# First layer: the heads' softmax denominators summed and inverted on 128 partitions and spread through DRAM

## What is computed

```python
x_flat = x.reshape(B, C, H * W).transpose(0, 2, 1)
Q, K, V = (split_heads(x_flat @ W + b) for W, b in ((Wq, bq), (Wk, bk), (Wv, bv)))
attn = softmax(einsum('bhnd,bhmd->bhnm', Q, K) * scale, axis=-1)
out = einsum('bhnm,bhmd->bhnd', attn, V)
out = out.transpose(0, 2, 1, 3).reshape(B, H * W, C) @ Wo + bo
y = out + x_flat
y = (y - mean(y)) / sqrt(var(y) + EPS) * gamma + beta      # over the channels
```

## Time and profile before

| | us |
|---|---|
| median of 3 runs | 5652.98 (5651.7 to 5654.66) |
| the profiled execution's own time | 5656.6 |
| its span, first to last instruction | 5654.8 |
| busy PE | 5338.5 (94% of the span) |
| busy DVE | 4949.7 (88%) |
| busy GpSimd | 4692.7 (83%) |
| busy ACT | 3876.3 (69%) |

### The profile page before, as it was taken

The page is one execution under the profiler, slowest core; times in us unless marked ns, Lnnn a source line. Parts: engine busy times, 40 slices in busy tenths (PEclk is TensorE's granted clock), DMA queues, the critical chain, the costliest instruction groups (busy, mean ns, idle before and its releaser), DMA issues. The chain is left out here.

```text
span 5654.8 us, 81519 instructions
## 1 busy us (share of the span) xinstructions
PE 5338.5 (94%) x25264; PEld 2432.7 (43%) x25264; DVE 4949.7 (88%) x7220; ACT 3876.3 (69%) x7513; POOL 4692.7 (83%) x3661
## 2 busy tenths in 40 slices
PE   7999999999999999999999999968888888888888
PEld 3444444444444444444444444423333333333333
DVE  6888888888888888888888888829999999999998
ACT  3666666666666766666666666657777777777776
POOL 4888887888888788888788888747888888888887
PEclk8999999999999999999999999989999999999999
DMA  4111122211111211112211010225555555555555
GB/s 139 36 53 50 37 61 71 60 55 38 46 49 64 79 39 53 45 40 62 64 54 33 18 32 21 67 84 196 186 190 188 188 187 189 186 188 190 186 188 174
DMA packets 337475, 549.14 MB, mean 97 GB/s; under 512 B 76016, under 2 KB 99568, under 8 KB 335600
## 3 DMA queue, kind: packets, MB, share of 16 engines
q1 hardware_dynamic: 327536, 526.62, 28.8%
q10 hardware_dynamic: 9504, 17.31, 1.1%
HBM read 415.10 MB, written 109.84 MB: 93 GB/s over the span
## 5 line engine op out<-in xcount | busy, mean ns | idle before, releaser
L649 DVE TENSOR_REDUCE mpart<-ps 128x1 f32<-128x512 f32 x4096 | 2539.1, 682 | 536.4 <-PE ps L406 535.8
L533 ACT ACTIVATE exps<-ps 128x512 f32<-128x512 f32 x4096 | 2146.8, 600 | 1139.8 <-PE ps L413 1114.1
L406 PE MATMUL ps<-k_st,q_ring 96*128 96x512 f32 x4096 | 1778.2, 435 | 20.2 <-DMA k_st<-qk_split 15.6
L413 PE MATMUL ps<-q_ring,k_st 98*128 98x512 f32 x4096 | 1621.5, 397 | 3.8 <-ACT exps L533 3.4
L1300 POOL TENSOR_TENSOR hc<-hh,c_rep 128x512 f32<-128x512 f32 x1024 | 1295.8, 1278 | 310.8 <-DVE hh L1269 291.8
L1269 DVE TENSOR_TENSOR_SCAN hh<-d_a,carry,ps 128x512 f32<-128x512 f32 x1024 | 1311.9, 1284 | 0.0
L622 POOL TENSOR_TENSOR held<-exps 128x512 f32<-128x512 f32 x768 | 987.7, 1311 | 359.9 <-ACT exps L533 359.9
L406 PEld LDWEIGHTS ps<-k_st,q_ring 96*128 96x128 f32 x4096 | 774.7, 189 | 1136.5 <-DVE mpart L649 685.2
L622 POOL TENSOR_TENSOR sums<-exps 128x512 f32<-128x512 f32 x896 | 1134.5, 1282 | 72.0 <-ACT exps L533 70.0
L424 PE MATMUL ps<-exps,v_ring 128*32 128x512 f32 x8192 | 1092.4, 605 | 0.0
L413 PEld LDWEIGHTS ps<-q_ring,k_st 98*128 98x128 f32 x4096 | 778.3, 190 | 139.7 <-ACT exps L533 18.0
(11 more groups left out here) (113 smaller groups left out, 3881.3 us busy)
## 6 DMA issues: line engine op xcount, KB each, us to landing
d_a<-dt_dram SPq DMA_DIRECT2D x1040, 256.0 KB
qk_split<-hilo SPq DMA_DIRECT2D x128, 256.0 KB, 2.3
out_dram<-out_sb SPq DMA_DIRECT2D x128, 256.0 KB, 2.0
heads_in<-out_dram SPq DMA_DIRECT2D x32, 1024.0 KB, 5.2
q_ring<-qk_split SPq DMA_DIRECT2D x384, 64.0 KB, 2.0
k_st<-qk_split SPq DMA_DIRECT2D x45, 512.0 KB, 7.4
dt_dram<-dt SPq DMA_DIRECT2D x33, 512.0 KB, 5.5
s_u<-lo_u ACTq DMA_DIRECT2D x66, 256.0 KB, 5.9
```

Source lines behind the costliest of these rows:

```text
L406: nc.tensor.matmul(d_bank(("max", m, t)), q_ring[0:PARTS, m % 4, 128 * i:128 * i + 128], k_st[0:PARTS, g % 2, chunk(kc)], start=True, stop ...
L413: nc.tensor.matmul(a_bank(("exp", n, t)), k_st[0:SHIFT, n // NCH % 2, 128 * t:128 * t + 128], q_ring[0:SHIFT, n % 4, :], start=True, stop= ...
L533: nc.scalar.activation(exps[:, u % EXPS, CH * half:CH * half + CH], a_bank(("exp", n, t)), ACT.Exp, scale=SCALE).then_inc(a_done, 1)
L649: nc.vector.tensor_reduce(mpart[:, m % 2, t % 4, t // 4:t // 4 + 1], d_bank(("max", m, t)), AX.X, ALU.max).then_inc(d_done, 1)
```

## The change

The denominators no longer go through `denom`, `sel_d` and PE. `store_den` writes a slot's four rows to a DRAM tensor `den_dram` in pieces of 16 columns. In a slot with f, `load_den` loads them as `den_in`, with the (head, piece) pair as the 128 partitions and 4 x 16 values in each. DVE sums the four parts and takes the reciprocal (`invert`, in quad v = 3, behind its quarter of `held`). SP stores the 128 x 16 result to `rec_dram`, waits until it has landed, and loads it to `recip` with each head's row repeated on its 32 partitions (`spread_rec`). PE's matmul and ACT's two activations go, and so does the key "den" in the ring `a_at`. ACT's copy of the denominators moves: it stands behind the first exp tile of quad v = 1, no longer behind the fourth, in all slots but the last.

```diff
-                if v == 4:
-                    add(a, ("den", f))
...
                 def store_den(n):
                     f = batch_of(n) * NCH + n % NCH
                     sp.wait_ge(den_read, n + 1)
-                    if f >= NCH:
-                        sp.wait_ge(a_ready, a_at["den", f - NCH] + 1)
-                    sp.dma_start(denom[row:row + 4, half, :], den_parts[::D, n % 2, :]).then_inc(den_stored[n % 2], 16)
+                    if f >= 2 * NCH:
+                        sp.wait_ge(den_loaded, 16 * (f - 2 * NCH + 1))
+                    sp.dma_start(den_dram[batch_of(n) % 2, n % NCH, n // NCH % HEADS, :, :, :].rearrange("k q l -> q k l"),
+                                 den_parts[::D, n % 2, :].rearrange("q (k l) -> q k l", k=32)).then_inc(den_stored[n % 2], 16)
+
+                def load_den(f):
+                    sp.wait_ge(den_stored[f % 2], 16 * (last_slot(f) // 2 + 1))
+                    if f:
+                        sp.wait_ge(den_summed, f)
+                    sp.dma_start(den_in[:, :, :], den_dram[f // NCH % 2, f % NCH, :, :, :, :].rearrange("h k q l -> (h k) q l")
+                                 ).then_inc(den_loaded, 16)
+
+                def spread_rec(f):
+                    sp.wait_ge(rec_ready, f + 1)
+                    if f:
+                        sp.wait_ge(recip_ready, 16 * f)
+                        sp.wait_ge(d_done, d_at["join", f - 1] + 1)
+                    sp.dma_start(rec_dram.rearrange("h (k l) -> (h k) l", k=32), rec[:, :]).then_inc(rec_stored, 16)
+                    sp.wait_ge(rec_stored, 16 * f + 16)
+                    sp.dma_start(recip[:, :], rec_dram.rearrange("h (o l) -> h o l", o=1).to_broadcast([HEADS, D, CH])).then_inc(recip_ready, 16)
...
-                def spread_den(f):
-                    row, half = den_rows(f)
-                    pe.wait_ge(den_stored[f % 2], 16 * (last_slot(f) // 2 + 1))
-                    a_room(("den", f))
-                    nc.tensor.matmul(a_bank(("den", f)), sel_d[row:row + 16, :], denom[row:row + 16, half, :],
-                                     start=True, stop=True).then_inc(a_ready, 1)
...
-                def reciprocal(f):
-                    ready(("den", f))
-                    if f:
-                        act.wait_ge(d_done, d_at["join", f - 1] + 1)
-                    nc.scalar.activation(recip[:, :], a_bank(("den", f)), ACT.Ln).then_inc(a_done, 1)
-                    act.wait_ge(a_done, a_at["den", f] + 1)
-                    nc.scalar.activation(recip[:, :], recip[:, :], ACT.Exp, scale=-1.0).then_inc(recip_ready, 1)
...
                             exp_tile(m, t)
+                            if v == 1 and t == 4 and n:
+                                read_den(n - 1)
...
-                        if v == 1 and 0 <= n - 1 < NS:
+                        if v == 1 and n == NS:
                             read_den(n - 1)
...
+                def invert(f):
+                    dve.wait_ge(den_loaded, 16 * f + 16)
+                    if f:
+                        dve.wait_ge(rec_ready, f)
+                    nc.vector.tensor_reduce(den[:, :], den_in[:, :, :].rearrange("p q l -> p l q"), AX.X, ALU.add).then_inc(den_summed, 1)
+                    dve.wait_ge(den_summed, f + 1)
+                    if f:
+                        dve.wait_ge(rec_stored, 16 * f)
+                    nc.vector.reciprocal(rec[:, :], den[:, :]).then_inc(rec_ready, 1)
+
                 def normalise(f):
                     ready(("join", f))
-                    dve.wait_ge(recip_ready, f + 1)
+                    dve.wait_ge(recip_ready, 16 * f + 16)
```

More of the change, by code:

```diff
@@ L147, in layer0 @@
     out_dram = nc.dram_tensor("out_dram", [2, HEADS, 128, L], F32, kind="Internal").ap()
+    den_dram = nc.dram_tensor("den_dram", [2, NCH, HEADS, 32, 4, CH // 32], F32, kind="Internal").ap()
+    rec_dram = nc.dram_tensor("rec_dram", [HEADS, CH], F32, kind="Internal").ap()
     d_at, a_at = ring_positions()
@@ L166, in layer0 @@
         sel_o = sb("sel_o", [128, D])
-        sel_d = sb("sel_d", [128, 128])
         ones_d = sb("ones_d", [128, D])
@@ L182, in layer0 @@
         mrow = sb("mrow", [4, 2, 2, 128], F32R)
-        denom = sb("denom", [128, 2, CH])
+        den_in = sb("den_in", [128, 4, CH // 32])
+        den = sb("den", [128, CH // 32])
+        rec = sb("rec", [128, CH // 32])
         den_parts = sb("den_parts", [128, 2, CH])
@@ L216, in _ @@
                         sp.dma_start(z_ext[b, :, at:at + W], z_sb[:, 0:W]).then_inc(loaded, 16)
-                sp.wait_ge(loaded, 16 * (12 + 2 * B))
+                sp.wait_ge(loaded, 16 * (11 + 2 * B))
             @block.gpsimd
@@ L229, in _ @@
                     nc.vector.memset(k_st[PARTS:128, buf, :].bitcast(F32), 1.0)
-                dve.wait_ge(loaded, 16 * (12 + 2 * B))
+                dve.wait_ge(loaded, 16 * (11 + 2 * B))
                 for r in range(0, 128, D):
@@ L246, in layer0 @@
                              "z_stored", "f_in", "h_in", "joined")]
+        (den_loaded, den_summed, rec_ready, rec_stored) = [
+            sem(s) for s in ("den_loaded", "den_summed", "rec_ready", "rec_stored")]
         q_in = [sem(f"q_in{i}") for i in range(4)]
@@ L264, in a_bank @@
             return ps[:, EXP_BANK + a_at[key] % 3, :]
-        def den_rows(f):
-            return 32 * (f % 4), f % NCH // 4
         with nc.Block() as block:
@@ L319, in store_den @@
                     f = batch_of(n) * NCH + n % NCH
-                    row, half = den_rows(f)
-                    row += 4 * (n // NCH % HEADS)
                     sp.wait_ge(den_read, n + 1)
-                    if f >= NCH:
-                        sp.wait_ge(a_ready, a_at["den", f - NCH] + 1)
-                    sp.dma_start(denom[row:row + 4, half, :], den_parts[::D, n % 2, :]).then_inc(den_stored[n % 2], 16)
+                    if f >= 2 * NCH:
[16 more added lines that the diff above has]
+                    sp.dma_start(recip[:, :], rec_dram.rearrange("h (o l) -> h o l", o=1).to_broadcast([HEADS, D, CH])).then_inc(recip_ready, 16)
                 def store_out(n):
@@ L372, in _ @@
                         store_max(n + 1)
+                    if f is not None:
+                        load_den(f)
                     if g is not None:
                         store_z(g)
+                    if f is not None:
+                        spread_rec(f)
                     if n < 0 and 0 <= n - PRE - 1 < NCH:
@@ L506, in _ @@
                         if f is not None:
-                            if v == 4:
-                                spread_den(f)
                             if v == 6:
@@ L600, in _ @@
                             affine(g)
-                        if f is not None and v == 4:
-                            reciprocal(f)
             @block.gpsimd
@@ L725, in _ @@
                         if f is not None:
+                            if v == 3:
+                                invert(f)
                             if v == 5:
@@ L732, in layer0 @@
         clear(nc, names)
-def denominators():
-    m = np.zeros((4, 32, HEADS, D), np.float32)
-    for h in range(HEADS):
-        m[:, 4 * h:4 * h + 4, h] = 1
-    return m.reshape(128, 128)
 ST = 16
@@ L1379 @@
     l0["ident"] = np.eye(128, dtype=np.float32)
-    l0["sel_den"] = denominators()
     w = host(i)
```

1 line of the change is left out of this document (removed).

## The result

| | before | after |
|---|---|---|
| median of the timed executions, us | 5653.55 (5650.15 to 5655.39, 6) | 5676.05 (5671.12 to 5682.51, 6) |
| ratio, with its 95% interval | | 1.0042 [1.0029, 1.0055] |
| the profiled execution, us | 5656.6 | 5674.78 |
| its span, us | 5654.8 | 5673.0 |

The change makes the kernel 0.42% slower, some 22 us. I had forecast 5648 us and a range of 5636 to 5667: the sign and the range are both wrong. One execution each of e11 and e14 took far longer than the others of the same kernel (6332.6 and 16210.8 us) and stands outside the ranges given for them; it moves their medians by less than 0.7 us. Each group of experiments has a median of the kernel before of its own, from 5652.51 to 5654.73 us, and each ratio is taken against that.

The account below looks back on a forecast made before the run. PE was taken to bound the first layer, DVE some quads; 29 x (0.39 - 0.10) = 8.4, plus 1.5 (n = 126), plus 0.4 (start), less 5.2 (tail): 5.1 us saved, forecast 5648 us, range 5636 to 5667.

Parts of the forecast that it names:

- a claim of "zero": ACT's copy of the denominators moved three exp tiles forward: no cost; if its cover is gone, 13 us over 128 slots.

Follow-up runs that it names:

- e11: e10 with the reciprocals' load cut into four DMAs of 32 partitions; 5647.77 us, ratio 0.9981.
- e14: The changed kernel, copy back behind v = 1's fourth exp tile, k loaded at n % NCH == 2, DVE's sum done twice; 5667.1 us, ratio 1.002.
- e2: The changed kernel with ACT's copy of the denominators back behind the fourth exp tile of v = 1; 5662.41 us, ratio 1.0018.
- e10: The changed kernel, copy behind t = 5, k loaded at n % NCH == 2, sums' load ahead of heads' in the last finish; 5652.58 us, ratio 0.9992.
- e5: e2 with the load of k issued behind the reciprocals' load in slots with f; 5665.89 us, ratio 1.0024.
- e15: e11 with k loaded every eighth slot from 0, but at slots 34, 66 and 98 in place of 32, 64 and 96; 5642.56 us, ratio 0.9981.

## What to carry to other kernels

Before an instruction is moved on one engine, list everything that shares the ring of buffers it delays, not only the tiles of its own kind; the rare users, here one product in 50 of the first 125 slots, are the ones that wait. A chain of small transfers can be as late as the largest transfer near it, ahead or behind, so read the queue in every kind of slot, and ask not whether a jam is new but whether its first reader now comes earlier. And where a claim of "zero" has a price written beside it, that price belongs in the range.

## What the runs showed of the hardware

- A short stop of PE can cost a second time. In slot 32 of the kernel after PE waited 2.12 us, and about 1 us after it went on the granted clock fell to 0.50 for 3.4 us; the slot lost 3.2 us against the 31.35 of most finish slots. In slot 64 a stop of 1.41 us was followed by 3.4 us at 0.50 as well. But in slot 64 of e2 and in slot 26 of e10 the clock stayed at 1.00 after stops of 1.47 and 1.51 us, so the length of the stop alone doesn't tell. In e5, where PE stood for 3.58 us, it was at 0.51 for 6.8 us right after:

```profile
1030.20:1037.00 6.80, 6.71 (x17) 2.97 (x18) 4.38 (x8) 1.19 (x2) 1.26 (x1) 0.51 0.14 34
```

  In slot 32 of e15, without a stop, the clock is 1.00 all through.
- A DMA on a quarter of the engines that was issued 0.6 us ahead of 1.5 MB took 8.9 us instead of 5.1 (e5, slot 32); being issued first gave it no priority. The same 256 KB in four DMAs, one behind the other, land in 3.5 us (e11, tail).
- A store of 8 KB to DRAM, waited for, lands 1.4 us after its issue when nothing is beside it and 4.4 us beside a load of 1 MB. By the Trainium skill ("DMA: Bandwidth & Descriptors", Anatomy of one DMA) about 2.0 us are fixed in a DMA that GpSimd issues. No run here has one; SP issued this store, and the whole of it took less.
- VectorE's reciprocal of 16 elements on 128 partitions takes 253 ns, as long as its sum of 64 (250 ns).
